# Two cross-attention layers in float32: projections, outputs and the shift's transpose in the column tiles of the values

## The reference

```python
# layer 0: 16 heads of 64, scores unscaled
h = layernorm(x) * gamma + beta
Q, K, V = h @ Wq, context @ Wk, context @ Wv
attn = softmax(einsum('bihd,bjhd->bhij', Q, K), axis=-1) * scale
x = x + einsum('bhij,bjhd->bihd', attn, V).reshape(B, NQ, INNER) @ Wo + bo
# layer 1: 16 heads of 32
xn = x * rsqrt(mean(x * x) + EPS_RMS) * norm_w
q, k, v = xn @ wq, split(encoder_out @ wkv)
q, k = rotate(q), rotate(k)          # rotary embedding, then each head to unit length
attn = softmax(einsum('bqhd,bkhd->bhqk', q, k) * sqrt(32), axis=-1)
return x + einsum('bhqk,bkhd->bqhd', attn, v).reshape(B, T_dec, D_Q) @ wout
```

## Time and profile before

| | |
|---|---|
| time, median of 3 runs | 3376.78 us (3375.62 to 3377.91) |
| the profiled execution | 3378.76 us, span 3376.9 us |
| TensorE, matmuls | 3157.1 us busy, 93%, 20448 instructions |
| TensorE, weight loads | 1614.6 us, 48%, 20448 instructions |
| VectorE | 2385.7 us, 71% |
| ScalarE | 1404.2 us, 42% |
| GpSimd | 502.6 us, 15% |

### The profile page before, as it was taken

One profiled execution on the slowest core, in us unless ns is written; L12 is line 12 of the kernel. 1 busy time (PEld: TensorE's weight loads), 2 busy tenths in 40 slices (PEclk: granted clock), 3 DMA queues, 4 the chain that ended last, 5 costly groups with the idle time before them and its releaser, 6 DMA issues.

```text
span 3376.9 us, 51123 instructions
## 1 busy us (share of the span) xinstructions
PE 3157.1 (93%) x20448; PEld 1614.6 (48%) x20448; DVE 2385.7 (71%) x2805; ACT 1404.2 (42%) x1728; POOL 502.6 (15%) x221
## 2 busy tenths in 40 slices
PE   5999999899899999889999999998999999999897
PEld 3555555444355554544344555454434455545442
DVE  3667666787776676678776766667877767666877
ACT  1333333456433333355643333335563333334555
POOL 1000002342000000334100000034410000013440
PEclk8999999999999999999999999999999999999999
DMA  3001000101111010011111010101112010000001
GB/s 108 18 21 25 22 23 15 57 22 39 43 49 25 21 24 21 21 55 25 32 55 41 21 25 21 24 14 58 26 32 71 21 27 21 25 21 21 18 14 36
DMA packets 178322, 105.88 MB, mean 31 GB/s; under 512 B 81453, under 2 KB 147117, under 8 KB 178089
## 3 DMA queue, kind: packets, MB, share of 16 engines
q1 hardware_dynamic: 178088, 102.60, 11.4%
HBM read 93.12 MB, written 9.42 MB: 30 GB/s over the span
## 4 chain that ended last, share of the span: by engine, by line
PE 83%; DVE 8%; issue 4%; ACT 3%; DMA 1%; SPq 1%; DVEq 0%; POOL 0%; ACTq 0%; POOLq 0%
PE o_acc L654 19%; PE scores L642 19%; PE work L680 14%; PE work L676 11%; PE work L700 10%; PE work L610 5%; DVE acc L797 4%; PE work L694 3%; ACT probs L727 2%; DVE tile_max L778 1%; PE work L684 1%; DVE resid L882 1%; DVE stats L817 1%; PE work L710 0%; PE work L689 0%
## 5 line engine op out<-in xcount | busy, mean ns | idle before, releaser
L727 ACT ACTIVATE probs<-scores 128x1024 f32<-128x1024 f32 x1024 | 995.8, 1023 | 501.2 <-PE scores L642 462.1
L778 DVE TENSOR_REDUCE tile_max<-work 128x2 f32<-128x1024 f32 x496 | 607.0, 1224 | 557.4 <-PE work L610 554.0
L797 DVE TENSOR_TENSOR acc<-acc,probs 128x1024 f32<-128x1024 f32 x768 | 984.8, 1305 | 20.2 <-ACT probs L727 0.2
L654 PE MATMUL o_acc<-probs,v_tok 128*64 128x512 f32 (+1 forms) x4096 | 778.1, 611 | 0.1
L914 POOL TENSOR_TENSOR inv<-sumsq,power 128x16 f32<-128x16 f32 x64 | 233.0, 3640 | 2110.5 <-DVE sumsq L863 2110.5
L700 PE MATMUL work<-wo,o_sum 128*128 128x512 f32 x768 | 429.6, 647 | 39.7 <-issue 27.6
L642 PE MATMUL scores<-q_high,k_high 32*128 32x512 f16 (+1 forms) x2048 | 311.4, 394 | 71.0 <-ACT probs L727 47.3
L654 PEld LDWEIGHTS o_acc<-probs,v_tok 128*64 128x64 f32 (+1 forms) x4096 | 165.4, 122 | 349.1 <-issue 334.4
L882 DVE TENSOR_TENSOR resid<-work,resid 128x512 f32<-128x512 f32 x384 | 261.4, 684 | 65.3 <-PE work L700 65.2
L642 PE MATMUL scores<-q_high,k_low 32*128 32x512 f16 (+1 forms) x2048 | 305.4, 385 | 0.0
L642 PE MATMUL scores<-q_low,k_high 32*128 32x512 f16 (+1 forms) x2048 | 304.5, 384 | 0.0
(11 more groups left out here) (77 smaller groups left out, 2662.6 us busy)
## 6 DMA issues: line engine op xcount, KB each, us to landing
recip<-rows_dram SPq DMA_DIRECT2D x380, 64.0 KB, 2.1
stage<-in_x_dram SPq DMA_DIRECT2D x8, 1024.0 KB, 6.3
wq<-in_L_xattn_Wq_dram SPq DMA_DIRECT2D x32, 256.0 KB, 2.8
resid<-in_x_dram SPq DMA_DIRECT2D x8, 1024.0 KB, 5.4
wo<-in_L_xattn_Wo_dram SPq DMA_DIRECT2D x32, 256.0 KB, 2.7
out_dram<-resid SPq DMA_DIRECT2D x8, 1024.0 KB, 4.3
wk<-in_L_xattn_Wk_dram SPq DMA_DIRECT2D x32, 192.0 KB, 2.6
wv<-in_L_xattn_Wv_dram SPq DMA_DIRECT2D x32, 192.0 KB, 2.6
```

What stands on the lines that cost most here:

```text
L654: mm = pe.matmul(o_acc[h * d:(h + 1) * d, :], v_tok[par][:, kt, h * d:(h + 1) * d], probs[:, unit_slot(t, n, kt, h // 2), h % 2, :], start ...
L727: act.activation(probs[:, no % RING, :, :], scores[:, unit_banks(t, n, kt, u), :], ACT.Exp, scale=(1.0, float(D1) ** 0.5 / QK_SCALE ** 2)[ ...
L778: dve.tensor_reduce(tile_max[:, qt, :, n:n + 1], maxima_banks(e), AX.X, ALU.max, negate=True).then_inc(dve_freed, 1)
L797: dve.tensor_tensor(a[:, heads, :], before, probs[:, unit_slot(t, n, kt, u), :, :], ALU.add).then_inc(add_ok, 1)
```

## The change

Each entry of the plan gets a width `cols`: the head's width of the turn in whose step it stands (64 or 32), and 128 in the first step, which belongs to no turn. The projections L676 and L680, the output projection L700 and the shift's transpose L684 are issued as 128/`cols` matmuls on as many column tiles, each with its part of the stationary operand and all with the same moving operand, one after the other within each chunk. The shift's transpose changes from F32R to float32, so `ident_r` and its cast on VectorE go, and TensorE's first wait (`consts_ok`) no longer stands behind the identity's transfer on VectorE. The transposes L689, L705 and L710, the scores, the row maxima, the values and the denominators stay as they are.

```diff
--- before.py
+++ after.py
@@ -58,6 +58,7 @@
         self.kind, self.t, self.i = kind, t, i
         self.full = self.act = self.dve = self.high = self.rope = None
         self.banks, self.before = (), ()
+        self.cols = P
 
 
 WORK = ("R", "T", "q", "k", "v", "kr", "qr", "kT", "qT", "den", "den_end", "out", "ct", "xt")
@@ -259,6 +260,8 @@
         lasts = [e for e in st.fill if e.kind in WORK][-1:]
         for e in in_order(st):
             items[e.kind, e.t, e.i] = e
+            if st.t is not None:
+                e.cols = WIDTH_OF[st.t]
             if e.kind not in WORK:
                 continue
             if e.kind == "R":
@@ -357,7 +360,6 @@
             return ctx.enter_context(nc.semaphore(name))
 
         ident = sb("ident", [P, P])
-        ident_r = sb("ident_r", [P, P], F32R)
         ones_r = sb("ones_r", [P, P], F32R)
         ones = [sb("ones_scaled", [P, D0]), sb("ones_plain", [P, D1])]
         cos = sb("cos", [P, TT, D1])
@@ -389,7 +391,7 @@
         den_t = sb("den_t", [P, G1, HT])
         recip_t = sb("recip_t", [P, G1, HT])
         tile_max = sb("tile_max", [P, HT, G0, 2])
-        neg_max = sb("neg_max", [P, HT, P], F32R)
+        neg_max = sb("neg_max", [P, HT, P])
         shift = [sb(f"shift{i}", [P, S], F32R) for i in range(2)]
         raw = [sb(f"raw_{n}", [P, TT, G1, D1]) for n in ("k", "q")]
         turned = [sb(f"turned{i}", [P, HT, G1, D1]) for i in range(2)]
@@ -599,6 +601,13 @@
                 for before in e.before:
                     wait_freed(pe, before)
 
+            def columns(e):
+
+                return [slice(c, c + e.cols) for c in range(0, P, e.cols)]
+
+            def part(t, r):
+                return slice(t * P + r.start, t * P + r.stop)
+
             def rowmax(e):
                 half, n, qt = e.i
                 claim(e)
@@ -673,15 +682,18 @@
                     src, n_c = (hT, XC) if e.kind[0] == "q" else (cT, CC)
                     if e.kind in ("q", "k"):
                         for c in range(n_c):
-                            mm = pe.matmul(w, wt[:, c, :], src[:, c, tokens(e.i)], start=(c == 0), stop=(c == n_c - 1))
+                            for r in columns(e):
+                                mm = pe.matmul(w[r, :], wt[:, c, r], src[:, c, tokens(e.i)], start=(c == 0), stop=(c == n_c - 1))
                     else:
                         for j in range(HT):
                             for c in range(n_c):
-                                mm = pe.matmul(w[:, tile(j)], src[:, c, tile(HT * e.i + j)], wt[:, c, :], start=(c == 0), stop=(c == n_c - 1))
+                                for r in columns(e):
+                                    mm = pe.matmul(w[r, tile(j)], src[:, c, part(HT * e.i + j, r)], wt[:, c, :], start=(c == 0), stop=(c == n_c - 1))
                 elif e.kind == "T":
                     pe.wait_ge(neg_max_ok, 2 * turn0_no(e.t) + e.i + 1)
                     for j in range(HT):
-                        mm = pe.matmul(w[:, tile(j)], neg_max[:, j, :], ident_r[:, :], start=True, stop=True)
+                        for r in columns(e):
+                            mm = pe.matmul(w[r, tile(j)], neg_max[:, j, r], ident[:, :], start=True, stop=True)
                 elif e.kind in ("kT", "qT"):
                     which = "kq".index(e.kind[0])
                     pe.wait_ge(scaled_ok, ITEM[e.kind[0] + "r", e.t, e.i].rope)
@@ -697,7 +709,8 @@
                     if e.i % HT == 0:
                         pe.wait_ge(o_norm_ok, half_no(e.t, n))
                         pe.wait_ge(w_in["o", par], 16 * (e.t // 2 + 1))
-                    mm = pe.matmul(w, o_sum[buffer_of(e.t, n)][:, tile(e.i % HT)], wo[par][:, :], start=True, stop=True)
+                    for r in columns(e):
+                        mm = pe.matmul(w[r, :], o_sum[buffer_of(e.t, n)][:, part(e.i % HT, r)], wo[par][:, :], start=True, stop=True)
                 elif e.kind == "ct":
                     src, done, value = context_tile(e.t, e.i)
                     pe.wait_ge(done, value)
@@ -899,9 +912,7 @@
             dve.memset(ones[0][:, :], float(D0) ** 0.5)
             dve.memset(ones[1][:, :], 1.0)
             dve.memset(ones_r[:, :].bitcast(F32), 1.0)
-            dve.memset(neg_max[:, :, :].bitcast(F32), 0.0)
-            dve.wait_ge(ident_in, 16)
-            dve.tensor_copy(ident_r[:, :], ident[:, :]).then_inc(consts_ok, 1)
+            dve.memset(neg_max[:, :, :], 0.0).then_inc(consts_ok, 1)
             dve.wait_ge(tables_in, 16 * 2)
             run(rowmax, lambda t, n, kt: None, added, entry, on_vector)
```

## The result

The changed kernel takes 3317.55 us (median of 4 runs, 3311.47 to 3320.79), the kernel before beside it 3377.35 (4 runs, 3375.62 to 3380.36): ratio 0.982, 95% interval 0.9803 to 0.9837. That is 60 us faster, inside the range of 3280 to 3346 and 15 us over the forecast of 3303. The profiled executions are 3378.76 us before and 3319.18 after (spans 3376.9 and 3317.4).

The account below looks back on a forecast made before the run. TensorE was taken to bound the kernel, nearly fully in the first layer, about 0.68 in the second. 94 - 28 + 8 + 11 = 85 us of TensorE, less 11, gave 74 off 3376.8: 3303 us, range 3280 to 3346.

Parts of the forecast that it names:

- Layouts, 94 us of TensorE: Fewer array layout changes between neighbouring matmuls, 1213 for 1695, save 94 us: about 64 first layer, 30 second.
- The seam's 0.10 and the load's 0.10: First layer: leaving o_acc for a full-width matmul costs 0.10 us for the layout change plus 0.10 for uncovered weight load.
- the seam stays: Rival: the 0.10 us belongs to any new operand or bank, not the layout; slower, 3394 us; chance 0.04.
- Passes of 512 at 0: k, q and out matmuls with 512 columns of data, split into side-by-side tiles, cost nothing extra.
- Passes of 128 at 0.110: v, kr and qr: 4096 tiled passes take 0.110 us each, lower bound 0.107, gaining 8 us.
- issue binds: Rival: v, kr, qr in four tiles limited by instruction issue, 54 ns a pair; about 3587 us; chance 0.08.
- the rule against it: Skill's 62 ns per matmul in the sequencer: four tiles take 248 ns a pass, some 350 us more in second layer.
- The shift's transpose, 28 us lost and 11 credited: 64 transposes in plain F32 need twice the passes, 28 us lost; 0.2 us in 56 steady halves covered, 11 us.
- the rival at 0.13: Rival: tiled passes take 0.13 us in the second layer, 0.114 in the first; 43 us less gain, 3346; chance 0.12.
- First layer, 50 us: TensorE's saving in the first layer, some 50 us, counted nearly in full because TensorE bounds it.
- Second layer, 0.68 of 35 us = 24: Second layer: of some 35 us saved on TensorE, 0.68 counts; 11 lost to exponentials and sums late next.
- The case in which the second layer gives nothing at all: Rival: sums, exponentials and the reciprocals' round trip bind the second layer; only 50 us gained, 3327; chance 0.18.

Follow-up runs that it names:

- experiment 3: The changed kernel with each layer's column tiles given the other layer's width (32 in the first, 64 in the second): 3369.11 us, ratio 0.9983.
- Experiment 4: The changed kernel with the shift's transpose back at full width in F32R: 3311.78 us, ratio 0.9814.
- Experiment 12: The changed kernel, shift's transpose at full width in F32R, a half's first output tile last only in first-layer halves where that had gained: 3301.53 us.
- 5: The kernel before, with VectorE's second-layer sums over 128 of 512 columns from the third key tile on: 3346.86 us, ratio 0.991.
- 6: The changed kernel, with VectorE's second-layer sums over 128 of 512 columns from the third key tile on: 3280.41 us, ratio 0.9711.
- 10: The kernel before, with second-layer sums and exponentials both cut to 128 of 512 columns from the third key tile on: 3317.12 us.
- 11: The changed kernel, with second-layer sums and exponentials both cut to 128 of 512 columns from the third key tile on: 3257.92 us.

## Why the prediction was right, and where not

*Layouts, 94 us of TensorE: right in kind and size.* The seam's 0.10 and the load's 0.10 went where forecast (1.77 and 0.86 us), and experiment 3, with tiles but not the common layout, brought the seam back and lost most of the gain. The rival "the seam stays" is out.

*Passes of 512 at 0: right.* *Passes of 128 at 0.110: measured 0.109*, near the lower bound. The rival "issue binds" is out, with 4 pairs of load and matmul in 0.109 us, 27 ns each; so is the rival at 0.13. Of the rule against it the prediction left out the condition: the Trainium skill ("TensorE: Matmul & The Clock Gate", section "Wait — 56ns, not 53.3ns?") gives the 62 ns for hardware decode turned off. The 27 ns agree that they do not bind here.

*The shift's transpose, 28 us lost and 11 credited: right.* Its step has three of my terms: 0.20 us for the output tile, 0.15 for the denominators, 0.20 for the transpose's own layout, against 0.43 of passes with 0.2 of idle time as cover, in all 0.32 us less; the step is 0.33 us shorter. Experiment 4 undoes the transpose's part and gains or loses nothing that could be told, as these terms add up to (0.20 against 0.43 less 0.2).

*First layer, 50 us: 46.3 measured, 43 with the clock taken out.* The steps with q, k and v gave 0.19 to 0.27 us each, as summed. What failed is that every layout change was counted as if nothing else were late. In the step with a half's first output tile, the multiplication of the outputs by VectorE is late, and I had read only a step without it. It gave 0.02 to 0.08 us of some 0.2, over some 50 halves 6 to 9 us. Experiment 12 frees it where that pays, and takes off more of its wait than the change had put there.

*Second layer, 0.68 of 35 us = 24: too high, and this is the step that failed.* It gave 14.8 us, 13 with the clock taken out. The factor was TensorE's share of the chain of waits, an average over steps with different limits. The savings do not fall evenly: a step with an output tile alone was already held to 3.15 us by the score banks, where TensorE needed 3.03, and gives nothing (its wait was too short for the timeline to print); a step with a projection gives all of its own. TensorE's idle time ahead of the scores rose by 6.5 us, and the stalls inside groups take 1.8. What the sums hold is not settled: 13 against 16 us in 5 and 6 is no more than the spread of such numbers. I named exponentials and sums as late next; what I lacked was the loop's length. The case in which the second layer gives nothing at all is out (3332.55 us with the first layer alone, 3317.55 with both).

*What stays open.* With sums and exponentials both cut, 20 of the 35 us come out, and 2.8 are in stalls. The traces place part of the last 12. The 15 steps with an output tile that still take 3.15 us hold 3.0. And in steps with the first output tile of a half TensorE stops ahead of that tile, 1.64 us in the step of 4.68 above. What it waits for there is VectorE's multiplication of the outputs, which comes behind the rotation of a projection. The changed kernel's timeline of VectorE, the rotation's start and the multiplication:

```profile
694.56 0.69 DVE L869 TENSOR_TENSOR raw_q<-work,cos 128x512 f32<-128x512 f32 x1 [1.69 <-ACT squares L766]
...
696.62 0.69 DVE L819 TENSOR_TENSOR o_sum<-o_sum,recip 128x512 f32<-128x512 f32 x1
```

The multiplication ends at 697.31, and out starts at 697.41. That step is as long in 10 and 11 (4.68 and 4.67 us). In the change, 16 steps with a half's first output tile (four in each batch element) gave about nothing, taken together, where the prediction's prices say 0.22 us each, 3.5 us in all. So not only exponentials and sums were late next, as the prediction had it, but this multiplication too. Moving it ahead of the rotation was not tried. Where the rest lies is open; the projections' copies and a too high price of the four-tile seams are left. Also not tried is whether shorter stops of TensorE would keep its clock up. The runs with the lower mean granted clock are mostly the longer ones of their kernel.

## What to carry to other kernels

A matmul with another array layout than its neighbour cost 0.10 us going in and, at full width, 0.10 for a weight load that nothing covers. Fill work put beside tiled work should take its tiles, even at twice or four times the instructions. Before crediting that, split the steps by what ends them: in a step that ends in a wait, the saving goes into the wait, also where the wait is too short to be printed. Then change the order in just those steps: a tile that waits for another engine goes last where the bank behind it is free early, and stays first where it is not.

## What the hardware showed that I had not expected

- Four column tiles of 32 with 128 columns of data sustain 4 MATMULs and 4 weight loads in 0.109 us over a run of 96 (712.89 above), 27 ns a pair, half of the 54 ns that bounded my rival.
- Stalls of 0.29 to 2.88 us without any wait, in kernels with many small matmuls, 2.2 to 2.5 us after a packet of 16384 bytes began on the instruction queue. The Trainium skill ("Runtime: NRT & Kernel Launch", section "Instruction fetch mechanics") says that fetching is hidden behind the sequencer's own pace; if the stalls are what they look like, the runs here do not agree where a pair comes every 27 ns, though the cost is 2 to 4 us in 3300.
- The lower clock came and went in stretches of 3.4 and 6.8 us, behind stops of TensorE of 1.2 us and more, at different places in every kernel: from 37 to 87 us in all of an execution, 24 to 34 of them in stretches that begin in the first 95 us. So a profiled execution alone can't tell 10 us. A wait of TensorE can cost twice, once itself and once by the clock behind it.
